# GNN of four layers on one core: when ACT copies the head sums after layer 2's gathers

## What is computed

```python
x = _layernorm(x + _L0_gnn_ref(x, edge_index, L0_gnn_W, L0_gnn_b))
x = _layernorm(x + _L1_gnn_ref(x, edge_index, edge_weight, ...))
x = _layernorm(x + _L2_gnn_ref(x, L2_gnn_W, L2_gnn_att, src, dst))
x = _layernorm(x + _L3_gnn_ref(x, edge_weight, L3_gnn_W, L3_gnn_b, src, dst))

# layer 2, 4 heads of 64 features
z = einsum('nd,hdf->nhf', h, W)
e = leaky_relu(es[src] + ed[dst], 0.01);  ex = exp(e - m[dst])
out = segment_sum(ex / denom[dst] * z[src], dst)
# layer 3
out = relu(segment_sum((h @ W)[src] * edge_weight, dst) + b)
```

## Time and profile before

| | |
|---|---|
| median of 3 runs | 2008.88 us (2003.04 to 2011.71) |
| the profiled execution | 2004.1 us, of which its span is 2002.2 us |
| PE busy in the span | 1748.5 us, 87% |
| DVE busy | 1274.0 us, 64% |
| ACT busy | 449.5 us, 22% |
| POOL busy | 673.2 us, 34% |
| mean granted clock of TensorE | 0.808 of full speed |

### The profile page before, as it was taken

One profiled execution on the slowest core, in us unless ns is written; L12 is line 12 of the kernel. 1 busy time (PEld: TensorE's weight loads), 2 busy tenths in 40 slices (PEclk: granted clock), 3 DMA queues, 4 the chain that ended last, 5 costly groups with the idle time before them and its releaser, 6 DMA issues.

```text
span 2002.2 us, 38284 instructions
## 1 busy us (share of the span) xinstructions
PE 1748.5 (87%) x13533; PEld 1503.9 (75%) x13533; DVE 1274.0 (64%) x2915; ACT 449.5 (22%) x1000; POOL 673.2 (34%) x567
## 2 busy tenths in 40 slices
PE   5668898888888999996689889998988877899998
PEld 5457777767776888885578778887877765788887
DVE  9678888888885112222788888888898876311212
ACT  0432322222321001002233332332333333100000
POOL 0122222222222000001777777777777800000000
PEclk9989999999999999998555555555555555899999
DMA  6102121212124344441333333333333330245441
GB/s 168 70 36 102 70 102 70 102 70 102 70 103 197 108 143 143 151 146 45 91 91 83 89 86 88 86 85 89 86 89 88 90 114 1 97 151 176 162 157 45
DMA packets 110199, 202.38 MB, mean 101 GB/s; under 512 B 70372, under 2 KB 87061, under 8 KB 100483
## 3 DMA queue, kind: packets, MB, share of 16 engines
q1 hardware_dynamic: 54851, 141.62, 20.1%
q0 software_dynamic: 55232, 59.15, 12.3%
HBM read 152.00 MB, written 53.36 MB: 103 GB/s over the span
## 4 chain that ended last, share of the span: by engine, by line
PE 57%; issue 23%; DVE 8%; DMA 4%; POOL 4%; ACT 2%; DVEq 1%; POOLq 0%; SPq 0%; ACTq 0%
PE bank L1224 27%; PE bank L1290 16%; PE bank L1281 4%; DMA ring<-edge_rows,cur 3%; PE bank L1264 2%; PE bank L1354 2%; POOL ring L450 2%; PE bank L1273 1%; PE bank L1232 1%; POOL ring L419 1%; DVE work L957 1%; PE bank L1177 1%; PE bank L1337 1%; ACT ring L593 1%; DMA ring<-attention_rows,work 1%
## 5 line engine op out<-in xcount | busy, mean ns | idle before, releaser
L450 POOL DMA_INDIRECT ring<-attention_rows,work x425 | 514.8, 1211 | 172.9 <-issue 143.4
L1290 PE MATMUL bank<-work,ring 125*65 125x48 f32 x3400 | 395.1, 302 | 0.0
L1290 PEld LDWEIGHTS bank<-work,ring 125*65 125x65 f32 x3400 | 387.7, 224 | 8.4
L1224 PE MATMUL bank<-big,ring 128*128 128x256 f32 x1250 | 273.0, 379 | 1.4 <-DVE x_sb L821 1.4
L1224 PE MATMUL bank<-big 128*128 128x256 f32 x1250 | 272.9, 379 | 0.0
L1224 PEld LDWEIGHTS bank<-big,ring 128*128 128x128 f32 x1250 | 236.5, 190 | 33.8 <-DVE x_sb L821 2.2
L1224 PEld LDWEIGHTS bank<-big 128*128 128x128 f32 x1250 | 236.6, 190 | 31.7
L1168 PE MATMUL bank<-big 128*128 128x256 bf16 x1875 | 209.0, 273 | 14.6 <-ACT big L493 14.6
L1168 PEld LDWEIGHTS bank<-big 128*128 128x128 bf16 x1875 | 181.4, 98 | 38.9 <-ACT big L493 18.3
L427 POOL MEMSET big<- 128x3200 f32 x25 | 69.2, 2770 | 355.3 <-DMA adjacency<-big 295.2
L1157 PE MATMUL bank<-work 128*128 128x100 bf16 x800 | 153.5, 210 | 33.4 <-DVE big L796 28.8
(11 more groups left out here) (204 smaller groups left out, 2153.8 us busy)
## 6 DMA issues: line engine op xcount, KB each, us to landing
adjacency<-big SPq DMA_DIRECT2D x25, 1600.0 KB, 5.2
ring<-adjacency SPq DMA_DIRECT2D x25, 1600.0 KB, 7.0
big<-adjacency SPq DMA_DIRECT2D x25, 1600.0 KB, 7.2
ring<-attention_rows,work POOLq DMA_INDIRECT x425, 3.9
edge_rows<-edge_list SPq DMA_DIRECT2D x1, 4983.0 KB
x_sb<-in_x SPq DMA_DIRECT2D x1, 3072.0 KB
out_x<-xnT SPq DMA_DIRECT2D x24, 128.0 KB, 4.3
attention_rows<-ring SPq DMA_DIRECT2D x13, 135.0 KB, 2.3
```

The lines of the kernel that those rows point to most:

```text
L450: G.indirect_dma_start(out=rows[0:EP, s, c, 0:ZG], out_offset=None, in_=ztab[:, :], in_offset=bass.IndirectOffsetOnAxis(ap=idx[:, s, c:c + ...
L1224: ins = mm(bank[:, 0:D], slots[s][:, b, :], ybuf[:, b, :], start=(b == 0), stop=(b == NT - 1))
L1290: ins = mm(sum_banks[three(s)][0:FH, h * WIN:(h + 1) * WIN], rows[0:EP, s, c, h * FH:(h + 1) * FH], prob[:, s % 2, c, h * WIN:(h + 1) * WI ...
```

## The change

ACT's loop over t only. The number of copies and their operands stay. Before, `stage(0)` stands ahead of the loop and turn t begins with `stage(t + 1)`. After, `stage(0)` to `stage(3)` stand ahead of the loop and turn t ends with `stage(t + 4)`. The wait inside `stage` is as it was.

```diff
@@ -593,10 +593,9 @@
                 S.copy(stg[0:FH, t % SLOTS], acc_h[0:FH, :, tile_cols(t)]).then_inc(e2["stg"], 1)
 
             act.wait_ge(y["added"], nsw * GROUPS + SLOTS)
-            stage(0)
+            for t in range(SLOTS - 1):
+                stage(t)
             for t in range(NT + 3):
-                if t + 1 < NT:
-                    stage(t + 1)
                 if 1 <= t <= NT:
                     deviation(e2, t - 1)
                 if 2 <= t <= NT + 1:
@@ -604,6 +603,8 @@
                 if t >= 3:
                     act.wait_ge(e2["z"], t - 2)
                     S.copy(ybuf[:, t - 3, :], rr_bank[:, 0:D]).then_inc(e2["y3"], 1)
+                if t + SLOTS - 1 < NT:
+                    stage(t + SLOTS - 1)
             for t in range(NT):
                 deviation(e3, t)
```

## The result

The changed kernel takes 1977.8 us (median of 4 runs, 1975.27 to 1981.44) against 2007.1 us before (4 runs). The ratio is 0.9855, 95% interval 0.9827 to 0.9883.

The account below looks back on a forecast made before the run. PE, at half clock and waiting for ACT's late copy, was taken to bound the stage at 3.80 us a step. DVE's 2.37 us pace and the tail gain 29.3 us, less 0.8: 28.5, forecast 1979 us, range 1971 to 1990.

Parts of the forecast that it names:

- The front: Stage start on ACT: two more early copies delay table load by 1.04 us, costing nothing; cover 0.8 us.
- The loop: ACT's cyclic order stays, copies run two tiles further ahead: PE finds them done, square root unmoved, slot wait costs zero.
- The pace: Layer 2's last stage: DVE sets 2.37 us a step, so its step 24 begins 26.7 us earlier.
- the sum ahead of its allowance: Stage through its tail: layer 3 starts near 1696.1 against 1725.43, 29.3 us earlier, before the half-clock deduction.
- The allowance for half clock: Stage's first gapless turns: PE's 2.85 us binds until the clock rises; 0.8 us deducted, leaving 28.5 us gain.
- step (3): What is late next: PE gapless at 2.85 us a turn; DVE's square-root wait shrinks from 1.28 to about 0.33 us.
- case (B): Rival, 12%: stage clock rises and falls again, 0.24 us a turn lost; gain 21 to 24 us, 1981 to 1988.
- The clock: Gapless PE work lifts TensorE's granted clock some 5 us into the gapless stretch, near 1646 to 1652, and it holds.
- I take that row: Clock holds despite PE's waits for DVE, as in layer 0's projection: 1.00 at 7.18 us busy of 10.
- PE's turn at half clock: PE's transposes and layer 3 weight product in the stage: 0.70+0.43+1.72 = 2.85 us a gapless turn.
- (A): Rival, 13%: clock stays at half in the stage, PE binds at 2.85 us; gain 16 to 19, 1985 to 1993.
- The median: Baseline choice: profiled execution gives 1975.6 us, shown median 2008.88 gives 1980.4; 1979 taken, nearer the median.

Follow-up runs that it names:

- first_lead4: Changed kernel, but the copy of tile t+4 stands first in turn t, ahead of ACT's square root; ratio 0.9849, stage 65.0 us.
- after_again: The changed kernel run once more, unaltered, on another chip where the attention loop's index loads were slower; ratio 0.9836, stage 65.0 us.
- before_fill: Kernel before, copy left late, plus one idle PE product in each turn where PE waits for the copy; ratio 0.9852, stage 67.7 us.
- attn_fill_again: Changed kernel plus one idle PE product in all attention-loop groups but the first, rerun on another chip; ratio 0.9776, loop 657.3 us.

## Why the prediction was right

The time came out at 1977.8 us against 1979, inside 1971 to 1990.

*The front.* Right. The table load ended at 1638.52, the square root at 1638.83, and DVE asked for it at 1639.66: 0.8 us of cover, as the prediction had it.

*The loop.* Right. The copy no longer stands in PE's way, the square root doesn't come later, and the wait for a free slot cost nothing, also in first_lead4, where it is a turn tighter. That one more turn of lead is enough was not said.

*The pace.* Right to the last digit: 2.374 us a step from tile 5 to tile 24, and 7.13 us from tile 24's start to layer 3 where the prediction had 7.05. The stage lost 29.26 us, and the sum ahead of its allowance was 29.3.

*The allowance for half clock.* Wrong: 0.8 us was taken off for the turns before the clock rises, and nothing was lost, since PE's lead over DVE carried it over them: tile 5's transposes were done at 1645.50, and DVE took them up at 1647.28. The wait of 0.33 us for the square root that step (3) expected at half clock never came. For the same reason case (B) was priced too high. The clock did rise and fall, as in (B), and 0.24 us a turn was charged for it. PE's turn at half clock is 2.57 us and not 2.85, 0.20 above DVE's 2.37, and a fall that lasts one or two turns takes less than the lead.

*The clock.* The rise was forecast, by the same sign, and came 13.5 us into the stage (15 to 21 were forecast). "Does the clock hold then? I take that row" failed: layer 0's projection held 1.00 at 7.18 us busy of 10, the stage with 3.35 of 5 did not. It didn't matter here, because DVE sets the step.

*PE's turn at half clock.* Mis-sized. The prediction added up 0.70+0.43+1.72 = 2.85 us from pieces of the chain, and the gapless turn took 2.57. The sum for the forecast did not use it, since it went by DVE's step, but (A) did: its 16 to 19 us would be about 22 with 2.57. Nor did the prediction see that the clock alone, with the copy left late, brings 26.6 us.

*The median.* The 1.2 us between 1979 and 1977.8 are the choice between two baselines, 2004.1 and 2008.9, and the 0.8 us above; runs of the kernel before lay between 2000 and 2014 us, except on the chip of after_again. That the medians differ by 29.3 us, as the stages of the two traces do, is luck to the tenth: what lies ahead of the stage moved these two executions by 3.34 us against each other.

## What to carry to other kernels

A copy into a ring of slots wants its lead counted in the consumer's turns: its place in the producer's loop is only where it is written. If it is needed right behind something that the producer itself waits for, one turn more takes it off the path, and further slots bring nothing. And a short wait of TensorE in each turn can cost more than its length: here PE waited 0.98 us a step (19.5 us in 20 waits), taking the wait away at half clock was worth 1.23, and filling it with an idle product, which brought the clock up, 1.27. Before shortening such a wait, fill it with an idle product into a free bank and see what the stage would take at full clock. Take the length of a gapless turn from starts in a timeline and not from the sum of its recorded pieces.

## What was not expected of the hardware

Idle TensorE work made the kernel faster twice: 26.6 us in the stage (before_fill), where each turn got one product of 128x256 in f32, and about 16 us in the attention loop (attn_fill_again), where each group but the first got one and the mean clock went from 0.53 to 0.66. The clock at half and gaps of only 0.98 us in 3.80 went together for 20 turns, some 76 us. DVE's scalar_tensor_tensor on 64 columns, with one operand in PSUM, took 0.86 us for four, nearly as much as two operations on 256 columns.
